# Decoder layer with a selective scan and an int8 feed-forward: gate and up weights measured beside in_proj, rounded inside the scan loop, and turned by transposing transfers

## The chip, the core and the metric

The kernel runs on one core of one Trainium2 chip. A core has TensorE (PE), VectorE (DVE), ScalarE (ACT), GpSimd (POOL), SyncE (SP), which here only issues transfers, and 16 DMA engines. The metric is the device time of one execution in microseconds; lower is better. Each engine runs its own list of instructions in the order in which the program emits them, and waits on semaphores.

## The reference

Two batches of 512 tokens, width 1024, go through three residual parts. Cut to what is computed:

```
# 1: x = x + mixer(layernorm(x))
u, gate = split(h @ W_in.T)                       # 2 x 2048 channels
u = silu(causal_conv4(u) + conv_b)
dt, B, C = split(u @ Wx.T); each rmsnorm'ed
delta = softplus(dt @ Wdt.T + dt_bias)
state = exp(delta * A) * state + (delta * u) * B  # along t, 2048 channels x 16 states
y = (sum_n state * C + u * D_param) * silu(gate)
out = y @ W_out.T
# 2: x = x + fake_quant(layernorm(x)) @ fake_quant(ctx)
# 3: x = x + ffn(layernorm(x)), every operand of a product int8:
s = max(max|t|, rows) / 127;  q = clip(round(t / s)) * s
h = silu(xq @ w_gate_q.T) * (xq @ w_up_q.T)       # 2752 hidden channels
out = h_q @ w_down_q.T
```

The scales of w_gate and w_up (2752 x 1024) are one per hidden channel, those of w_down (1024 x 2752) one per output channel.

## The kernel before

Everything is in channels-by-time tiles of 128 partitions. `mixer` (L42) first normalises the eight token tiles (`ln_stats` L841, `ln_apply` L850 on VectorE), TensorE turns them (L392), and ScalarE and VectorE copy them out (`ln_evac` L598, L855). Then TensorE computes the u half of in_proj of batch 0, 16 chunks of 128 channels of 16 passes each (`u_part` L396); ScalarE applies the first tap of the convolution (L610), VectorE the other three (`conv_rest` L861), ScalarE the silu of a group of four chunks (`u_silu` L618), and TensorE the small product with Wx (`ssm_product` L428), which sits in its list between passes for the gate (`gate_part` L461).

The scan loop has eight groups (two batches of four groups of four chunks) of 16 steps, one per state. In a step ScalarE makes exp(delta*A) (`decay` L652), GpSimd delta*u*B (`times_b` L770), VectorE runs the recurrence along time (`scan` L926), TensorE turns the states (`turn_state` L486), and VectorE (`add_states` L933) or ScalarE and GpSimd (L664, L789) add them up, weighted by C. In between, by step numbers written into the loops, come the rest of in_proj of both batches, the silu of the gate (`silu_gate` L680 to L683, two loads of tables), and the output product. SP loads u back (`load_u` L256, two buffers) and the rows of B (`load_b` L262, a ring of four).

`attend` (L1001) does the second part in staggered stages. In its last two stages it also computes the scales and codes of the first two chunks of w_gate and w_up: loads L1167, maxima `weight_scales` L1440, codes `weight_codes` L1297.

`feed_forward` (L1473) loops over 22 chunks of 128 hidden channels. For a chunk, SP loads both weight tiles (L1606); VectorE takes the row maxima and scales (`scales` L1816), ScalarE the rounded codes (`codes` L1738: the large number ROUND is added, which leaves the integer in the low bits), TensorE turns them in blocks of 128x128 into four PSUM banks (`turn` L1644), and ScalarE and VectorE copy them out to bf16 with ROUND taken off (`copy_out` L1594). The products are 32 passes of 512 columns (`products` L1665), in two banks for the gate and two for up. VectorE scales them (`scale_products` L1836), ScalarE does the silu (L1753), GpSimd the product (L1793), ScalarE the absolute value (`size` L1758), VectorE the running peak (`raise_peak` L1848). The eight row tiles of w_down are taken along in the same way, in three pieces each (`scales_d` L1828, `codes_d` L1745), through one buffer `raw_d`. A short chain behind the loop turns the peaks into the hidden scales; then the hidden values are rounded chunk by chunk, batch 0 on VectorE (L1893, L1897), batch 1 scaled on GpSimd (L1798) and rounded on VectorE, and TensorE runs the down product of batch 0 with all eight banks open (L1712) and that of batch 1 (L1729).

The places of w_down's tiles in the loop are set by a formula, so is the split of the copies:

```
first = t * (OC - 2) // (JT - 1)      # tile t of w_down: piece 0 at chunk first,
wd_at[first] += [(t, 0)]              # pieces 1 and 2 at the next
return u % 3 == 2                     # this copy-out on VectorE, else on ScalarE
```

## Time and profile before

| | us |
|---|---|
| time, median of 3 executions (1770.48 to 1774.33) | 1770.86 |
| the profiled execution's own time | 1774.07 |
| its span | 1772.3 |
| 0 to 186: layer norm, in_proj of batch 0 | 186 |
| 186 to 1171: scan loop | 985 |
| 1171 to 1416: output product, attend | 245 |
| 1416 to 1669: feed-forward loop and the chain behind it | 253 |
| 1669 to 1772: down product | 103 |

Over the span TensorE is busy 1453 us, VectorE 1387, GpSimd 969, ScalarE 848. A stage is bound by the engine that is busy nearly all of it, or by a chain that passes through several; a total says little here, since the stages have different limits. The granted TensorE clock is 0.92 of full on average.

### The profile page before, as it was taken

Reading aid. Unit: us, or ns where it says so; the run is one execution under the profiler, and the core shown is the slowest. Engines: PE = TensorE matmul, PEld = TensorE weight load, DVE = VectorE, ACT = ScalarE, POOL = GpSimd, SP = SyncE. Lnnn points to the kernel's source line nnn. Section 1 sums busy time; section 2 is a strip of 40 time slices with the busy share of each in tenths; the row PEclk is TensorE's granted clock in tenths of the full one; section 3 lists DMA queues with packets and bytes.
Section 4 is the critical chain, followed back from the end, with each engine's and each line's share of the span. In section 5 each row is a group of like instructions: output and inputs, shape, how many; then the busy total and the mean of one; then the engine's idle time right before and its main releaser. Section 6 shows DMA issues by size and latency. Waiting matters only on the chain. (4 is left out here: it accounts for less than half of the span.)

```text
span 1772.3 us, 18711 instructions
## 1 busy us (share of the span) xinstructions
PE 1453.4 (82%) x5879; PEld 774.0 (44%) x5912; DVE 1386.7 (78%) x1748; ACT 847.9 (48%) x1213; POOL 969.1 (55%) x793
## 2 busy tenths in 40 slices
PE   5999578778789877688888887888999379999788
PEld 3444334444444444444444444443444255555333
DVE  4423899989989999999999898953674658888684
ACT  1212556565566446566465565532322467878200
POOL 0000979879779778898988898930000012222530
PEclk8999788989989989679999899998999689999889
DMA  4343221431321321324616516626520234352004
GB/s 152 95 150 128 85 72 54 129 107 36 129 102 58 107 73 41 102 66 160 220 48 213 176 64 212 238 101 231 201 69 27 74 137 178 127 183 92 24 0 166
DMA packets 73676, 205.15 MB, mean 116 GB/s; under 512 B 6800, under 2 KB 24336, under 8 KB 68784
## 3 DMA queue, kind: packets, MB, share of 16 engines
q1 hardware_dynamic: 70416, 188.29, 31.4%
q10 hardware_dynamic: 3168, 15.73, 2.4%
q8 instruction: 46, 0.75, 0.2%
q14 instruction: 46, 0.38, 0.1%
HBM read 176.66 MB, written 27.33 MB: 115 GB/s over the span
## 5 line engine op out<-in xcount | busy, mean ns | idle before, releaser
L931 DVE TENSOR_TENSOR_SCAN hbuf<-decay,hbuf 128x512 f32<-128x512 f32 x512 | 610.7, 1208 | 37.7 <-ACT decay L661 37.7
L661 ACT ACTIVATE decay<-delta,chan_sb 128x512 f32<-128x512 f32 x512 | 350.2, 688 | 414.6 <-DVE hbuf L931 413.7
L499 PE MATMUL turn<-ident,hbuf 128*128 128x128 f32 x2048 | 349.2, 302 | 200.7 <-DVE hbuf L931 164.8
L499 PEld LDWEIGHTS turn<-ident,hbuf 128*128 128x128 f32 x2048 | 262.4, 154 | 478.8 <-DVE hbuf L931 243.0
L945 DVE SCALAR_TENSOR_TENSOR acc<-turn,pn,acc 128x512 f32<-128x512 f32 x360 | 261.9, 728 | 27.5 <-PE turn L499 26.1
L789 POOL TENSOR_TENSOR acc<-acc,part 128x512 f32<-128x512 f32 x120 | 153.1, 1276 | 57.8 <-ACT part L671 57.5
L1793 POOL TENSOR_TENSOR hid<-gs,us 128x512 f32 (+1 forms) x44 | 56.2, 1284 | 194.6 <-ACT gs L1753 181.8
L770 POOL TENSOR_TENSOR hbuf<-wout,sx 128x512 f32<-128x512 f32 x128 | 158.7, 1274 | 0.4 <-POOL wout L778 0.2
L770 POOL TENSOR_TENSOR hbuf<-du,b_more 128x512 f32<-128x512 f32 x128 | 158.9, 1276 | 0.0
L770 POOL TENSOR_TENSOR hbuf<-wout,b_more 128x512 f32<-128x512 f32 x128 | 158.6, 1273 | 0.0
L770 POOL TENSOR_TENSOR hbuf<-du,sx 128x512 f32<-128x512 f32 x128 | 158.5, 1273 | 0.0
L1675 PE MATMUL bank<-codes,wT 128*128 128x512 bf16 (+1 forms) x683 | 153.8, 382 | 1.3 <-ACT wout L1736 0.2
L481 PE MATMUL bank_g<-wout,codes 128*128 128x512 f32 x256 | 136.9, 622 | 0.0
L413 PE MATMUL bank_u<-wout 128*128 128x512 f32 x224 | 118.8, 652 | 0.9 <-DVE wout L858 0.9
L1325 POOL TENSOR_TENSOR rstd<-rstd,mhalf 128x1 f32<-128x1 f32 x16 | 12.9, 807 | 175.4 <-DVE rstd L1364 175.4
L1675 PEld LDWEIGHTS bank<-codes,wT 128*128 128x128 bf16 (+1 forms) x704 | 69.8, 99 | 79.7 <-issue 3.2
L413 PE MATMUL bank_s<-wout 128*128 128x512 f32 x208 | 100.3, 598 | 0.0
L481 PE MATMUL bank_s<-wout,codes 128*128 128x512 f32 x192 | 100.1, 603 | 0.0
L812 POOL TENSOR_TENSOR rs<-rs,mhalf 128x12 f32<-128x12 f32 x2 | 4.5, 2272 | 147.4 <-DVE rs L898 147.4
L671 ACT ACTIVATE part<-turn,pn 128x512 f32<-128x512 f32 x120 | 80.2, 668 | 6.3 <-PE turn L499 6.3
L796 POOL TENSOR_TENSOR y_out<-y_out,gbuf 128x512 f32<-128x512 f32 x32 | 40.6, 1269 | 70.9 <-DVE y_out L923 64.0
L1184 PE MATMUL bank_o<-wout,codes 128*128 128x512 f32 x128 | 58.0, 614 | 3.9 <-PEq L53 3.9
(208 smaller groups left out, 2173.2 us busy)
## 6 DMA issues: line engine op xcount, KB each, us to landing
wout<-in_woutT SPq DMA_DIRECT2D x48, 512.0 KB, 4.2
codes<-in_wg SPq DMA_DIRECT2D x8, 2048.0 KB, 7.7
sx<-bt_scratch SPq DMA_DIRECT2D x64, 256.0 KB, 3.2
b_more<-bt_scratch SPq DMA_DIRECT2D x64, 256.0 KB, 3.4
raw_d<-in_w_down SPq DMA_DIRECT2D x8, 1376.0 KB, 5.7
wout<-in_w_gate SPq DMA_DIRECT2D x21, 512.0 KB, 4.1
wout<-in_w_up SPq DMA_DIRECT2D x21, 512.0 KB, 4.8
wout<-in_wu SPq DMA_DIRECT2D x18, 512.0 KB, 3.5
```

The lines of the kernel that those rows point to most:

```text
L413: last = pe.matmul(u_bank(i)[:, :], w_ring[:, i % 2, k * P:k * P + P], xT[:, k, b * L:b * L + L], start=(k == 0), stop=(k == KC - 1))
L481: mm = pe.matmul(gate_bank(G, j)[:, :], wg_buf[:, k, j * P:j * P + P], xT[:, k, b * L:b * L + L], start=(k == 0), stop=(k == KC - 1))
L499: last = pe.transpose(turn[t % 2][:, j * P:j * P + P], hbuf[:, s % 4, j, t * P:t * P + P], ident[:, :])
L661: act.activation(decay_bank[q % 2][:, :], delta[:, G % 2, j, :], ACT.Exp, scale=a_col(GD * (G % GROUPS) + j, n)).then_inc(dA_done, 1)
L671: act.activation(part[:, k % 2, :], turn[ZT % 2][:, :], ACT.Copy, scale=pn[:, G // GROUPS, ZT, c:c + 1]).then_inc(part_done, 1)
L770: pool.tensor_tensor(hbuf[:, s % 4, j, :], du[G % 2][:, j, :], b_row[s % 4], ALU.mult).then_inc(dbu_done, 1)
L789: pool.tensor_tensor(a, a, part[:, k % 2, :], ALU.add).then_inc(part_added, 1)
L931: dve.tensor_tensor_scan(h, decay_bank[q % 2][:, :], h, 0.0, ALU.mult, ALU.add).then_inc(scan_done, 1)
L945: dve.scalar_tensor_tensor(a, state, pn[:, G // GROUPS, t, c:c + 1], a, ALU.mult, ALU.add)\
L1184: last = pe.matmul(bank_o[w % 2][half][:, :], (keep.yT if w < 2 else yT)[:, w % 2, c, :], wout[:, c, half * 512:half * 512 + 512], start=( ...
L1675: last = pe.matmul(banks[b][0:r, :], wT[:, c % 2, m, k, 0:r], keep.codes[:, k, b * L:b * L + L], start=(k == 0), stop=(k == KC - 1))
L1793: pool.tensor_tensor(hid[0:r, bass.ds(c, 1), b * L:b * L + L], gs[0:r, b:b + 1, :], us[0:r, b:b + 1, :], ALU.mult)\
```

## The change

1. In `mixer`, the first VectorE copies of the turned tiles come before the statistics of tiles 4 to 7.
2. The row maxima of all 44 tiles of w_gate and w_up (22 chunks, two matrices) are taken by VectorE between the convolution taps of batch 0 (`weight_max`), from raw tiles that SP loads through a ring of eight, and all scales are computed there at once.
3. In the scan loop ScalarE rounds these tiles, each in four pieces of 128x512, two that scale and add ROUND and two that take it off into bf16. SP loads each raw tile a second time and stores the bf16 codes to a scratch in memory. To make room, u has one buffer instead of two and is loaded twice a group, and the rows of B have a ring of three.
4. `attend` loses its weight work; at its end SP issues eight transposing transfers, four chunks of two matrices, of 128x1024 bf16 each.
5. The feed-forward loop has no turns on TensorE. Weights arrive turned, four chunks ahead. The product banks alternate between two sets of four. Tiles of w_down are measured at chunk `wd_at`, rounded one iteration of the loop later, made plain bf16 another one later, and turned by one transposing transfer from SBUF to SBUF, behind which the next tile's load stands on SP.
6. The rounding of batch 1 of the hidden values moves from VectorE to ScalarE.

```
+        def units_at(i):
+            at = [2, 0, 2, 2] + [4] * 9 + [2]
+            lo = sum(at[:max(i - 1, 0)])
+            return range(lo, lo + at[i - 1]) if 1 <= i < DC - 1 else range(0)
...
+        QSLOTS = 2 * (STEPS - 8)
+
+        def quant_at(q):
+            return range(4 * UNITS * q // QSLOTS, 4 * UNITS * (q + 1) // QSLOTS) if q < QSLOTS else range(0)
...
+            def load_raw(u):
+                m, c, n = u % 2, u // 2, unit_rows(u)
+                if u >= RAWS:
+                    sp.wait_ge(w_scale, u - RAWS + 3)
+                else:
+                    sp.wait_ge(stat, 4 * (u + 1))
+                sp.dma_start(raw[u % RAWS][0:n, :], (w_gate, w_up)[m][c * P:c * P + n, :]).then_inc(raw_in[u % RAWS], 16)
...
+            def load_quant(u):
+                m, c, n = u % 2, u // 2, unit_rows(u)
+                if u >= 2:
+                    sp.wait_ge(q_step, 4 * (u - 1))
+                else:
+                    sp.wait_ge(w_scale, W_DONE)
+                sp.dma_start(qraw[0:n, u % 2, :], (w_gate, w_up)[m][c * P:c * P + n, :]).then_inc(q_in[u % 2], 16)
...
+            def store_quant(u):
+                m, c, n = u % 2, u // 2, unit_rows(u)
+                sp.wait_ge(q_step, 4 * (u + 1))
+                sp.dma_start(wq_dram[m, c * P:c * P + n, :], qcode[0:n, :]).then_inc(q_stored, 16)
```

In ScalarE's part of the mixer, with the two calls in its loop over steps:

```
+            def quant(q):
+                for o in quant_at(q):
+                    u, half, plain = o // 4, o % 2, o % 4 >= 2
+                    n, c = unit_rows(u), u // 2
+                    v = qraw[0:n, u % 2, half * 512:half * 512 + 512]
+                    if plain:
+                        act.wait_ge(q_step, o - 1)
+                        if u >= 1:
+                            act.wait_ge(q_stored, 16 * u)
+                        act.activation(qcode[0:n, half * 512:half * 512 + 512], v, ACT.Identity, bias=rnd[0:n, 1:2])\
+                            .then_inc(q_step, 1)
+                    else:
+                        act.wait_ge(q_in[u % 2], 16 * (u // 2 + 1))
+                        if u == 0:
+                            act.wait_ge(w_scale, W_DONE)
+                        act.activation(v, v, ACT.Identity, bias=rnd[0:n, 0:1], scale=keep.iw[0:n, u % 2, c:c + 1])\
+                            .then_inc(q_step, 1)
...
+                    quant(2 * s)
...
+                    quant(2 * s + 1)
```

VectorE's part of the mixer:

```
+            def weight_max(u):
+                n = unit_rows(u)
+                dve.wait_ge(raw_in[u % RAWS], 16 * (u // RAWS + 2))
+                dve.tensor_reduce(keep.am[0:n, u % 2, u // 2:u // 2 + 1], raw[u % RAWS][0:n, :], AX_X, ALU.max,
+                                  apply_absolute_value=True).then_inc(w_scale, 1)
+
             for i in range(TT):
                 ln_stats(i)
             for i in range(TT):
                 ln_apply(i)
+            for i in range(TT):
+                ln_evac(2 * i + 1)
             for i in range(TT, TOK // P):
                 ln_stats(i)
-            for i in range(TT):
-                ln_evac(2 * i + 1)
+            dve.memset(rnd[:, 0:1], ROUND)
...
+                        for u in units_at(GD * g + j):
+                            weight_max(u)
                     if g >= 1 and j == 1:
                         add_ssm(g - 1)
+            dve.wait_ge(w_scale, UNITS + 2)
+            dve.tensor_scalar(keep.sw, keep.am, 1.0 / QMAX, SMIN, ALU.mult, ALU.max).then_inc(w_scale, 1)
+            dve.wait_ge(w_scale, UNITS + 3)
+            dve.reciprocal(keep.iw, keep.sw).then_inc(w_scale, 1)
             add_ssm(GROUPS - 1)
```

The feed-forward: the places of w_down, SP, and the order of an iteration on ScalarE and VectorE.

```
+        wd_at = {c: t for t, c in enumerate((0, 3, 6, 9, 11, 14, 17, 20))}
...
+            def load_wT(c):
+                sp.wait_ge(up_mm, 2 * (c - WT) + 2)
+                r = rows(c)
+                for m in range(2):
+                    sp.dma_start(wT[:, c % WT, m, :, 0:r], wq_dram[m, c * P:c * P + r, :], transpose=True)\
+                        .then_inc(wT_load[c % WT], 16)
+
+            def turn_wd(t):
+                sp.wait_ge(wd_plain, NP * (t + 1))
+                if t == 0:
+                    sp.wait_ge(pad_made, 1)
+                sp.dma_start(wdT[:, 0:OC, t * P:t * P + P], code_d[:, :], transpose=True).then_inc(wd_turned, 16)
 
             def load_wd(t):
                 if t >= 1:
-                    sp.wait_ge(block_turned, of["d", t - 1, NP - 1][-1] + 1)
+                    sp.wait_ge(wd_plain, NP * t)
                 sp.dma_start(raw_d[:, :], w_down[t * P:t * P + P, :]).then_inc(wd_load, 16)
...
+                if c + WT < OC:
+                    load_wT(c + WT)
+                if c - 2 in wd_at:
+                    turn_wd(wd_at[c - 2])
+                    if wd_at[c - 2] + 1 < JT:
+                        load_wd(wd_at[c - 2] + 1)
+            turn_wd(JT - 1)
...
+            def plain_d(t, m):
+                act.wait_ge(wd_code, NP * t + m + 1)
+                if m == 0 and t >= 1:
+                    act.wait_ge(wd_turned, 16 * t)
+                act.activation(code_d[:, piece(m)], raw_d[:, piece(m)], ACT.Identity, bias=rnd[:, 1:2]).then_inc(wd_plain, 1)
...
-                if 1 <= c <= OC:
-                    for b in range(BATCH):
+                    if 1 <= c <= OC:
                         silu(c - 1, b)
+                if c - 1 in wd_at:
+                    for m in range(NP):
+                        codes_d(wd_at[c - 1], m)
+                if c - 2 in wd_at:
```

ScalarE's rounding of batch 1 of the hidden values, for each chunk:

```
+                act.wait_ge(q_scaled[1], c + 1)
+                act.activation(v, v, ACT.Identity, bias=rnd[0:r, 0:1]).then_inc(q_rounded, 1)
+                act.wait_ge(q_rounded, c + 1)
+                to = q_space(c - 1, 1)[0:r] if c else q0[0:r, 1:2, :]
+                act.activation(to, v.unsqueeze(1), ACT.Identity, bias=rnd[0:r, 1:2]).then_inc(q_done[1], 1)
```

On VectorE, at the end of in_proj of batch 0: the taps of chunks 13 and 14 (line L868 before, L968 now), with the ssm sum of a group. Before:

```order
L868 SCALAR_TENSOR_TENSOR wout<-bank_s,chan_sb,wout 128x511 [waits conv_start]
L868 SCALAR_TENSOR_TENSOR wout<-bank_s,chan_sb,wout 128x510 [waits conv_tap]
L868 SCALAR_TENSOR_TENSOR wout<-bank_s,chan_sb,wout 128x509 [waits conv_tap]
L878 TENSOR_TENSOR ssm_sum<-bank_m,ssm_sum 96x512 [waits ssm_added,ssm_mm]
L868 SCALAR_TENSOR_TENSOR wout<-bank_g,chan_sb,wout 128x511 [waits conv_start]
L868 SCALAR_TENSOR_TENSOR wout<-bank_g,chan_sb,wout 128x510 [waits conv_tap]
L868 SCALAR_TENSOR_TENSOR wout<-bank_g,chan_sb,wout 128x509 [waits conv_tap]
L868 SCALAR_TENSOR_TENSOR wout<-bank_u,chan_sb,wout 128x511 [waits conv_start]
```

Now, with maxima of weight tiles (L1051), the next rows after chunk 13's taps:

```order
L968 SCALAR_TENSOR_TENSOR wout<-bank_s,chan_sb,wout 128x510 [waits conv_tap]
L968 SCALAR_TENSOR_TENSOR wout<-bank_s,chan_sb,wout 128x509 [waits conv_tap]
L1051 TENSOR_REDUCE row_scales<-du 128x1 [waits x_in6]
L1051 TENSOR_REDUCE row_scales<-du 128x1 [waits x_in7]
L1051 TENSOR_REDUCE row_scales<-acc 128x1 [waits x_in0]
L1051 TENSOR_REDUCE row_scales<-acc 128x1 [waits x_in1]
L978 TENSOR_TENSOR ssm_sum<-bank_m,ssm_sum 96x512 [waits ssm_added,ssm_mm]
L968 SCALAR_TENSOR_TENSOR wout<-bank_g,chan_sb,wout 128x511 [waits conv_start]
L968 SCALAR_TENSOR_TENSOR wout<-bank_g,chan_sb,wout 128x510 [waits conv_tap]
L968 SCALAR_TENSOR_TENSOR wout<-bank_g,chan_sb,wout 128x509 [waits conv_tap]
L1051 TENSOR_REDUCE row_scales<-acc 64x1 [waits x_in2]
L1051 TENSOR_REDUCE row_scales<-acc 64x1 [waits x_in3]
```

The four maxima behind chunk 13's taps stand ahead of the ssm sum and of chunk 14's, and two more behind those.

On ScalarE, steps around the silu of a gate in the scan loop. Before (decay L661, silu L682, scaled state L671):

```order
L661 ACTIVATE decay<-delta,chan_sb 128x512 [waits delta_done,scan_done] x2
L661 ACTIVATE decay<-delta,chan_sb 128x512 [waits scan_done] x2
L671 ACTIVATE part<-turn,pn 128x512 [waits part_added,turned]
L682 ACT_TABLE_LOAD
L682 ACTIVATE gbuf<-gbuf 128x2048 [waits gate_evac]
L683 ACT_TABLE_LOAD
L661 ACTIVATE decay<-delta,chan_sb 128x512 [waits scan_done] x8
L671 ACTIVATE part<-turn,pn 128x512 [waits part_added,turned]
L610 ACTIVATE wout<-bank_u,chan_sb 128x512 [waits ssm_mm,u_stored,w_used]
```

Now (decay L757, silu L778, scaled state L767, the pieces of weight rounding L709 with ROUND added and L703 with it taken off):

```order
L757 ACTIVATE decay<-delta,chan_sb 128x512 [waits delta_done,scan_done] x2
L703 ACTIVATE qcode<-wout,rnd 128x512 [waits q_stored,q_step]
L757 ACTIVATE decay<-delta,chan_sb 128x512 [waits scan_done] x2
L767 ACTIVATE part<-turn,pn 128x512 [waits part_added,turned]
L778 ACT_TABLE_LOAD
L778 ACTIVATE gbuf<-gbuf 128x2048 [waits gate_evac]
L779 ACT_TABLE_LOAD
L757 ACTIVATE decay<-delta,chan_sb 128x512 [waits scan_done] x2
L709 ACTIVATE wout<-wout,rnd,row_scales 128x512 [waits q_in0]
L757 ACTIVATE decay<-delta,chan_sb 128x512 [waits scan_done] x2
L709 ACTIVATE wout<-wout,rnd,row_scales 128x512 [waits q_in0]
L757 ACTIVATE decay<-delta,chan_sb 128x512 [waits scan_done] x2
```

The pieces stand between pairs of decays, one a half step, three times in four.

On SP, the beginning of the feed-forward. Before:

```order
L1614 DMA raw_d<-in_w_down 128x2752
L1609 DMA wout<-in_w_gate 128x1024 [waits block_turned]
L1609 DMA wout<-in_w_up 128x1024 [waits block_turned]
L1614 DMA raw_d<-in_w_down 128x2752 [waits block_turned]
L1609 DMA wout<-in_w_gate 128x1024 [waits block_turned]
L1609 DMA wout<-in_w_up 128x1024 [waits block_turned]
L1609 DMA wout<-in_w_gate 128x1024 [waits block_turned]
L1609 DMA wout<-in_w_up 128x1024 [waits block_turned]
```

Now:

```order
L1683 DMA raw_d<-in_w_down 128x2752
L1671 DMA_TRANSPOSE wout<-wq_scratch 128x8x128 [waits up_mm]
L1671 DMA_TRANSPOSE wout<-wq_scratch 128x8x128
L1671 DMA_TRANSPOSE wout<-wq_scratch 128x8x128 [waits up_mm]
L1671 DMA_TRANSPOSE wout<-wq_scratch 128x8x128
L1671 DMA_TRANSPOSE wout<-wq_scratch 128x8x128 [waits up_mm]
L1671 DMA_TRANSPOSE wout<-wq_scratch 128x8x128
L1678 DMA_TRANSPOSE wout<-code_d 128x22x128 [waits pad_made,wd_plain]
L1683 DMA raw_d<-in_w_down 128x2752 [waits wd_plain]
```

A load of w_down stands behind the turning transfer of the tile before it, and both behind the turned weights of four chunks ahead.

## Rows read from the trace of the kernel before

**Rows 1.** Busy times by stage; share of DMA engines and GB/s last.

```profile
core 0: us, PE busy (x) PEld busy (x) DVE busy (x) ACT busy (x) POOL busy (x), PEclk, DMA share, GB/s
...
186.00:1171.00 985.00, 785.63 (x3160) 432.98 (x3160) 915.25 (x1021) 554.61 (x826) 847.51 (x687) 0.91 0.34 112
...
1416.20:1669.00 252.80, 222.84 (x1251) 136.96 (x1274) 198.94 (x291) 181.00 (x256) 58.55 (x46) 0.95 0.37 131
```

**Rows 2.** Timeline at the start: start, duration, instruction, idle before it and releaser.

```profile
15.78 1.28 DVE L844 BATCH_NORM_STATS2 stats<-hbuf 128x6 f32<-128x512 f32 x2
...
22.28 0.68 DVE L858 COPY wout<-turn 128x512 f32<-128x512 f32 x1
...
23.02 1.11 PE L392 MATMUL turn<-ident,hbuf 128*128 128x128 f32 x4 [4.68 <-DVE wout L858]
...
26.71 2.05 PE L413 MATMUL bank_u<-wout 128*128 128x512 f32 x2 [0.87 <-DVE wout L858]
```

**Rows 3.** Busy times of two stretches, and the timeline at in_proj's end.

```profile
30.00:165.00 135.00, 135.00 (x340) 60.71 (x339) 43.77 (x61) 25.08 (x27) 0.00 (x0) 0.99 0.36 122
...
1176.00:1190.00 14.00, 13.27 (x32) 5.81 (x31) 0.00 (x0) 5.43 (x5) 1.26 (x1) 1.00 0.79 300
...
140.44 2.32 DVE L868 SCALAR_TENSOR_TENSOR wout<-bank_u,chan_sb,wout 128x511 f32<-128x511 f32 x3 [14.93 <-ACT wout L610]
...
156.44 1.91 ACT L618 ACTIVATE wout<-wout 128x2048 f32<-128x2048 f32 x1 [2.38 <-DVE wout L868]
...
159.95 3.60 PE L433 MATMUL bank_m<-wout,wx_buf 128*96 128x512 f32 x8
```

**Rows 4.** VectorE's waits for decay in the scans (total, times, longest), and one.

```profile
DVE hbuf L931 <- ACT decay L661: 37.7, 33, 3.2
...
450.20 1.22 DVE L931 TENSOR_TENSOR_SCAN hbuf<-decay,hbuf 128x512 f32<-128x512 f32 x1 [2.81 <-ACT decay L661]
```

**Rows 5.** Timeline of VectorE at the end of attend.

```profile
1406.56 2.33 DVE L1444 TENSOR_REDUCE row_scales<-wout 128x1 f32<-128x1024 f32 x2
```

**Rows 6.** Groups of the feed-forward loop: busy, mean ns, idle before.

```profile
L1675 PE MATMUL bank<-codes,wT 128*128 128x512 bf16 x651 | 146.8, 382 | 1.3 <-ACT wout L1736 0.2
...
L1657 PE MATMUL bank<-ident,wout 128*128 128x128 f32 x336 | 43.4, 286 | 2.3 <-DVE wout L1859 2.3
...
L1820 DVE TENSOR_REDUCE row_scales<-wout 128x1 f32<-128x1024 f32 x38 | 44.3, 1208 | 0.0
...
L1846 DVE SCALAR_TENSOR_TENSOR us<-bank,row_scales,sx 128x512 f32<-128x512 f32 x42 | 31.3, 744 | 13.0 <-PE bank L1675 13.0
...
L1855 DVE TENSOR_TENSOR wout<-wout,us 128x512 f32<-128x512 f32 x42 | 27.2, 687 | 2.9 <-ACT us L1758 2.9
...
L1830 DVE TENSOR_REDUCE amd<-raw_d 128x1 f32<-128x2752 f32 x8 | 24.0, 3004 | 3.8 <-DMA raw_d<-in_w_down 3.8
...
L1748 ACT ACTIVATE raw_d<-raw_d,rnd,isd 128x1024 f32<-128x1024 f32 x16 | 19.7, 1234 | 13.0 <-DVE isd L1834 13.0
```

**Rows 7.** DMA: issues, KB, landing time; then the queue from 1194 to 1202.

```profile
raw_d<-in_w_down SPq DMA_DIRECT2D x8, 1376.0 KB, 5.7
...
yT_scratch<-y_out SPq DMA_DIRECT2D x4, 256.0 KB, 2.3
...
q1 hardware_dynamic: 2036, 1.02, 43.5%
```

**Rows 8.** The last peak, and the first down product after it.

```profile
1658.82 0.69 DVE wout L1855
...
1669.04 3.19 PE L1712 MATMUL bank<-wout,q 128*128 128x512 bf16 x7 [3.77 <-DVE q L1897]
```

**Rows 9.** The chain and the timeline while hidden values are rounded.

```profile
1666.66 32.90 POOL L1798 TENSOR_TENSOR hid<-hid,wout 128x512 f32 x22 [8.54 <-ACT wout L1786]
...
1674.32 1.76 DVE hid L1893
...
1700.13 27.86 PE L1712 MATMUL bank<-wout,hid 128*128 x120 [2.58 <-DVE hid L1897]
```

374 lines of the change are left out of this document (147 added, 227 removed).

## The prediction, made before the changed kernel ran

> **What bounds the kernel now.** I read the busy times by stage first. From 186 to 1171 us the scans on VectorE set the time: 915 of 985 us busy, ScalarE 555, GpSimd 848. In the feed-forward loop, 1416 to 1669, TensorE is busy 223 of 253 us, with VectorE (199) and ScalarE (181) close behind [rows 1]. In in_proj, ahead of the scans, TensorE alone is full, and VectorE has 44 us of work in 135 [rows 3]. So work leaves the stage where three engines are full, and lands in one full on TensorE alone and in one full on VectorE. Next I read the timelines of the places where the edits sit, then the waits within the scans, then the groups of the loop.
>
> **Start.** TensorE is idle for 4.68 us before its turning at 23.02, released by VectorE's copy at 22.28; that copy stands behind sixteen statistics instructions of tiles 4 to 7, which begin at 15.78 [rows 2]. The new order puts the four copies first, at 15.9 instead of 22.3, and the statistics beside the products. The first product (26.71) comes about 6 us earlier; behind it the next thing late would be its weights, whose loads are issued with the inputs. **-6** (0 to -6.5).
>
> **In_proj.** VectorE gets 44 row maxima. One of 1024 columns takes 1.21 us [rows 6], so 53 us, and the stretch has 91 us free on VectorE, while TensorE has no gap [rows 3]. On average it fits. At the end it doesn't: conv_rest of chunks 12 and 13 begins at 140.44 (2.32 a chunk), u_silu starts at 156.44 as chunk 15's taps end and takes 1.91, and ssm_product stands at 159.95 behind gate passes [rows 3]. In the new order VectorE still has, from 140.44, four chunks' taps, ten maxima and the addition of one ssm sum (0.7): 140.44 + 4 x 2.32 + 10 x 1.17 (their pace back to back) + 0.7 = 162.1, silu to 164.0, ssm_product at 164.1, 4.1 us late. Three of gate_part's steps instead of one follow it, two more of 0.86, +1.7. So +6. A lag of VectorE carried from earlier groups and transfers come on top. Four raw tiles and one of in_proj's, 0.524 MB each, in a chunk's 6.86 us are 382 GB/s; the busiest stretch that I found moved 300 GB/s at a DMA share of 0.79, that is 380 at a full one [rows 3]. The weights of in_proj queue behind the raw tiles on one queue. I take +3 for this (0, as VectorE paces the raw loads, to 20, if nine chunks run at two thirds of their speed). **+9** (6 to 27).
>
> **Scan loop.** ScalarE gets 176 pieces of 128x512. ScalarE's codes_d takes 1.23 us for 1024 columns [rows 6], so 0.62 a piece and 109 us, and ScalarE has 430 us free there [rows 1]. The pieces lie between decays. VectorE waits 33 times for a decay, 37.7 us in all; the worst are at silu_gate, 2.81 us at 450.20 [rows 4]. A piece ahead of the awaited decay lengthens such a wait by at most 0.62. Three quarters of the half steps have a piece, so 33 x 0.62 x 0.73 = 15 if none is absorbed, and new short waits beside. **+10** (3 to 20). What hides the rest is ScalarE's idle time, and its pieces are issued behind decays of the same step, which are ready first. The loads and stores (22 + 11 MB over 900 us) are nothing for the queues; with a three-deep b_row ring a transfer still has two steps, of 985/128 = 7.7 us, ahead of its use.
>
> **Attend.** VectorE's maxima of the last stage, 2.33 us at 1406.56, stand between the last statistics and the last normalising [rows 5]; GpSimd's rstd covers 0.8 of it. **-2** (-1 to -3). The eight transposing transfers (0.26 MB each) stand on SP ahead of store_x2(7), where four raw loads of 0.52 MB stood. At 2.3 us, as y_out's stores of 0.26 MB [rows 7], eight cost what the four did, so nothing; if each were 2 us longer the last store and the stage's end would wait.
>
> **Feed-forward loop.** TensorE loses its turns of the gate and up weights (43.4 us) and of w_down, and keeps the products: 146.8 us in 651 of 704 passes, 7.0 or less a chunk, 154 in all [rows 6]. If the rest kept up, the loop would go down to that. It doesn't, because w_down goes round in a ring of one buffer: load, maximum, codes one iteration later, plain codes another iteration later, turning transfer, and the next load is issued behind that transfer on the same queue. VectorE stands in the next maximum until the load lands, and all iterations stand with it. One round:
> load 5.7 [rows 7]; maximum 3.0 and two small ones 0.4; the next chunk's two peaks and four scalings (2 x 0.69 + 4 x 0.74), 4.4, of which 3.3 are ahead of ScalarE's last silu of 0.6, so 3.9; codes_d 3.3 (2752 columns at 1.23 per 1024); the chunk after 4.5 (4.4 and a lag); plain_d 3.4, priced like it; issue 0.4; turning transfer T; semaphores' lags 0.8, an estimate [rows 6, 7]. That is 25.4 + T.
> T is the cost no row shows. It moves 0.72 MB. As a plain transfer by bytes it is 5.7 x 0.72/1.41 = 2.9. By packets: 256-byte pieces are 2816, 176 for each of 16 engines; the stores of y_out in 512-byte packets cost 0.435 x 16 x 8 us / 2036 = 27.4 ns each [rows 7], which gives 4.8. Below, 0 if it hides under the load. I take 3.0, the nearer row in size of transfer, and keep 0 and 4.8, and ten or more for smaller pieces.
> The Trainium skill (Advanced Engine Details and Errata, X-Bar Transpose) says that on trn2 transposing DMAs are as fast as plain ones; with the row of 5.7 us that is the 2.9 above. No run here shows it yet.
> Seven rounds of 28.4 are 199, 3 ahead of the first, and 24 from the last load's issue to the last peak (5.7 + 3.4, two chunks of 7.0 and their silu): 226. The chain behind the last peak (turning peaks, inverse, spreading, first codes) stays 9.5, from 1659.51 to 1669.04 [rows 8]. 236 against 252.8 [rows 1]: **-17**. It moves with T by 8 us a microsecond (eight transfers): -41 at 0, -3 at 4.8.
> Without the PE's pauses GpSimd's multiply and VectorE's peak stand closer in time and share their lock: I add **+3** (0 to 6).
>
> **Down.** GpSimd's 22 scalings of batch 1 take 32.90 us, 1.50 each, and meanwhile VectorE's multiply of 128x512 lasts 1.76 us where its maximum of two such tiles takes 0.69 [rows 6, 9]: each of VectorE's three instructions a chunk waits out one of GpSimd's, 4.5 us a chunk. With batch 1's rounding on ScalarE there are two, 3.0 a chunk: by GpSimd's end 11 chunks are done instead of 7, and the PE's 120 remaining passes at 232 ns [rows 9] are fewer by 3.7 x 8 = 29, 6.9 us; a bit more at the start. **-8** (-3 to -12). ScalarE's pieces for batch 1 (1.2 a chunk) keep pace with GpSimd and are done long before 1728.
>
> **Sum.** -6 + 9 + 10 - 2 - 17 + 3 - 8 = -11. The profiled execution took 1774.07 (span 1772.3), 3.2 above the median of 1770.86. 1774.07 - 11 = 1763 on its own scale, 1760 on the median's. I say 1761.
>
> **Rivals.**
> 1. Turning transfers are dear (ends slower). Loop and total move by 8 x (T - 3.0), so the whole gain is gone at T = 4.4. At 4.8 (27.4 ns for 256 bytes) the total is +3; at pieces of 128 bytes for the same 27.4 ns T is 9.6 and the total +42, 1813. For it: the packet price hardly falls with size in the rows. Against: nothing in the rows shows this kind of transfer. 0.22, around 1790.
> The Trainium skill's page VectorE: DVE Perf Modes (The three transpose paths) gives 1309 ns for one 128x128 block by DMA and advises TensorE where the result may go to PSUM. By it, if blocks did not overlap, T would be an estimated 29 us; no run here shows it, and it is the case of rival 2.
> 2. The 128x128 blocks run one after the other, each near what a small transfer takes here (2.3 us for 256 KB [rows 7], about 1 for 32 KB). 16 a chunk and 22 a piece of w_down on one queue are 22 x 16 + 8 x 22 = 528 us, the total +280, 2040. 0.03.
> 3. The mixer gives it back: the transfers of in_proj bind (27 instead of 9) and the pieces go fully onto VectorE's waits (20 instead of 10). -11 + 28 = +17, 1788. For it: 382 GB/s wanted of 380. Against: VectorE's own pace throttles the raw loads. 0.16.
> 4. The round is shorter, the transfer running beside the next load and the iterations overlapping: 25 us a round, another -24, 1737 to 1740. For it: the queue serves 16 engines and 5.7 us include a fixed part. 0.12.
> 5. The terms cancel, T near 4: 1767 to 1774. 0.07.
>
> **Numbers.** My forecast, 1752 to 1768, has 0.40. What a measurement can tell from no change is 0.2%, 3.5 us. Faster: 0.36 of the forecast, 0.12 of 4, 0.02 of 5: 0.50. Same: 0.04 + 0.05 of 5 + 0.01 of 3: 0.10. Slower: 0.22 + 0.03 + 0.15: 0.40. The range leaves out 1813 and the upper part of rival 1, rival 2, and little below: 1738 to 1803.
>
> **What would show it.** First product at about 20.5 instead of 26.7. ssm_product of the last group within 5 to 8 us of 160 + 4 - 6. Stage of the scans 988 to 1005 us, VectorE's wait for decay 41 to 58. Each w_down round 27 to 30, VectorE's idle ahead of the w_down maximum named DMA, one turning transfer about 3 us from issue to landing. Loop 236, TensorE idle a third of it. Batch 0's codes at 3.0 us a chunk. I am wrong if a turning transfer takes over 4.4 us, if SP is busy long with issuing one, or if TensorE waits for wT instead of VectorE for w_down.

## The result: 0.9% slower, and where the 12.3 us of the span went

The changed kernel takes 1787.94 us (median of 4, 1786.22 to 1794.10), the kernel before takes 1772.59 (median of 4). The ratio is 1.0092, 95% interval 1.0061 to 1.0123. I had forecast 1761, 11 us faster than before; faster had a chance of 0.50, slower 0.40. The time lies inside my range, but on the slower side.

The profiled execution of the changed kernel spans 1784.6 us (1786.35 its own time), 12.3 more than before's. Busy times by stage, as in [rows 1], cut at the same events (first scan, end of the scans, issue of the first load of w_down, first down product):

```profile
core 0: us, PE busy (x) PEld busy (x) DVE busy (x) ACT busy (x) POOL busy (x), PEclk, DMA share, GB/s
0.00:188.20 188.20, 154.47 (x400) 71.47 (x400) 117.97 (x164) 40.88 (x52) 12.29 (x16) 0.98 0.69 251
188.20:1188.80 1000.60, 791.14 (x3160) 434.57 (x3160) 915.96 (x1021) 670.44 (x1002) 848.28 (x687) 0.90 0.45 151
1431.30:1687.80 256.50, 179.66 (x744) 79.39 (x744) 138.00 (x166) 102.09 (x142) 57.90 (x47) 0.86 0.45 107
1687.80:1784.60 96.80, 81.24 (x352) 33.78 (x352) 64.81 (x74) 30.68 (x44) 31.83 (x21) 0.98 0.22 76
```

Against [rows 1]: in the scans VectorE's work is the same (916 against 915) in 16 us more; in the feed-forward all three engines have less to do, TensorE 180 instead of 223, and the stage is nevertheless 3.7 us longer. A stage in which every engine is idle for a good part is set by a chain of waits. By events, the span's difference is this sum:

| stage | forecast | measured |
|---|---|---|
| start (its effect on the first scan, from the run with this part alone, below) | -6 | -8.4 |
| in_proj, to the first scan | +9 | +10.6 |
| scans, first to last | +10 | +15.6 |
| attend | -2 | -2.7 |
| feed-forward loop and its chain | -14 | +3.7 |
| down | -8 | -6.5 |
| sum | -11 | +12.3 |

Two terms are off by much: the scans by 5.6 us and the feed-forward by 17.7, of 23.3 in all. The chain of waits there, one round of a w_down tile (start, us, what):

```profile
1489.39 3.31 SPq L1678
1492.69 0.04 issue
1492.74 6.35 DMA raw_d<-in_w_down
1499.08 0.02 issue
1499.11 3.03 DVE amd L1855
...
1502.43 0.70 DVE wout L1880
...
1503.26 0.76 DVE gs L1868
...
1504.05 0.63 ACT gs L1792
1504.67 0.53 ACT us L1797
...
1505.23 1.41 DVE wout L1880
...
1507.55 0.63 ACT gs L1792
1508.18 3.13 ACT raw_d L1781 x3
1511.30 0.53 ACT us L1797
1511.83 0.02 issue
1511.86 0.70 DVE wout L1880
...
1517.50 2.95 ACT code_d L1787 x3
1520.45 0.02 issue
1520.47 3.31 SPq L1678
```

The round is the predicted one in kind: load, maximum, codes, plain codes, turning transfer, load. The eight maxima start at 1437.6 to 1654.6, so seven rounds take 217.0 us, 31.0 each, not 28.4. By parts:

| part of a round | forecast | measured |
|---|---|---|
| load | 5.7 | 6.35 |
| maximum with its small ones | 3.4 | 3.25 |
| from there to the codes | 3.9 | 5.7 |
| codes | 3.3 | 3.1 |
| from there to the plain codes | 4.5 | 6.2 |
| plain codes | 3.4 | 2.95 |
| issue and turning transfer | 3.4 | 3.35 |
| lags | 0.8 | 0.1 |

The two iterations in between are what I mis-sized, by 3.5 us a round; the rows show why. Peak (L1880), scaling (L1868), silu (L1792) and absolute value (L1797) follow each other to and fro between VectorE and ScalarE, since the absolute value lies in the buffer that the next scaling overwrites; I had added VectorE's instructions as if they ran back to back. I call this to and fro the handshake. And each second peak takes 1.41 us, twice the 0.69 of [rows 6]. GpSimd's multiply runs beside just that one: a round earlier, the peak of the same place starts at 1483.56 and takes 1.42 us, and GpSimd's multiplies are these:

```profile
1483.15 1.27 POOL L1833 TENSOR_TENSOR hid<-gs,us 128x512 f32<-128x512 f32 x1 [4.64 <-ACT gs L1792]
1486.65 1.27 POOL L1833 TENSOR_TENSOR hid<-gs,us 128x512 f32<-128x512 f32 x1 [2.23 <-ACT gs L1792]
```

### The profile page after: what moved, and what is told of

It reads as the page before. It is cut to its first block and busy times, and to the rows that moved or that the text cites. A ratio compares the mean times of both kernels' runs of the same rounds, so it can differ in the third digit from the quotient of the medians.

```text
span 1784.6 us, 17613 instructions
## 1 busy us (share of the span) xinstructions
PE 1407.0 (79%) x5384; PEld 714.3 (40%) x5384; DVE 1363.5 (76%) x1642; ACT 911.0 (51%) x1314; POOL 970.5 (54%) x794
## 3 DMA queue, kind: packets, MB, share of 16 engines
q1 hardware_dynamic: 152208, 247.54, 42.8%
## 5 line engine op out<-in xcount | busy, mean ns | idle before, releaser
L757 ACT ACTIVATE decay<-delta,chan_sb 128x512 f32<-128x512 f32 x512 | 348.6, 687 | 318.8 <-DVE hbuf L1031 317.3
L1045 DVE SCALAR_TENSOR_TENSOR acc<-turn,pn,acc 128x512 f32<-128x512 f32 x360 | 263.0, 731 | 29.2 <-PE turn L577 27.8
L868 POOL TENSOR_TENSOR hbuf<-du,sx 128x512 f32<-128x512 f32 x172 | 213.1, 1275 | 2.0 <-DMA sx<-bt_scratch 2.0
L868 POOL TENSOR_TENSOR hbuf<-wout,sx 128x512 f32<-128x512 f32 x172 | 213.4, 1277 | 0.4 <-POOL wout L878 0.2
L1724 PE MATMUL bank<-codes,wout 128*128 128x512 bf16 (+1 forms) x704 | 171.1, 407 | 52.6 <-DVE gs L1868 51.6
L1833 POOL TENSOR_TENSOR hid<-gs,us 128x512 f32<-128x512 f32 (+1 forms) x44 | 55.8, 1269 | 187.2 <-ACT gs L1792 187.2
L1724 PEld LDWEIGHTS bank<-codes,wout 128*128 128x128 bf16 (+1 forms) x704 | 71.7, 104 | 151.9 <-issue 82.1
L491 PE MATMUL bank_u<-wout 128*128 128x512 f32 x224 | 111.8, 618 | 3.3 <-DMA wout<-in_wu 2.4
L1434 POOL TENSOR_TENSOR rstd<-rstd,mhalf 128x1 f32<-128x1 f32 x16 | 12.9, 807 | 174.8 <-DVE rstd L1473 174.8
L868 POOL TENSOR_TENSOR hbuf<-du,b_more 128x512 f32<-128x512 f32 x84 | 104.4, 1278 | 0.0
L868 POOL TENSOR_TENSOR hbuf<-wout,b_more 128x512 f32<-128x512 f32 x84 | 104.3, 1279 | 0.0
L1792 ACT ACTIVATE gs<-gs 128x512 f32<-128x512 f32 (+1 forms) x44 | 27.6, 630 | 135.6 <-DVE gs L1868 135.6
L1880 DVE TENSOR_TENSOR wout<-wout,us 128x512 f32<-128x512 f32 (+1 forms) x44 | 45.3, 1030 | 65.6 <-ACT us L1797 65.6
L767 ACT ACTIVATE part<-turn,pn 128x512 f32<-128x512 f32 x120 | 80.3, 669 | 6.3 <-PE turn L577 6.3
```

Source lines behind the costliest of these rows:

```text
L491: last = pe.matmul(u_bank(i)[:, :], w_ring[:, i % 2, k * P:k * P + P], xT[:, k, b * L:b * L + L], start=(k == 0), stop=(k == KC - 1))
L757: act.activation(decay_bank[q % 2][:, :], delta[:, G % 2, j, :], ACT.Exp, scale=a_col(GD * (G % GROUPS) + j, n)).then_inc(dA_done, 1)
L767: act.activation(part[:, k % 2, :], turn[ZT % 2][:, :], ACT.Copy, scale=pn[:, G // GROUPS, ZT, c:c + 1]).then_inc(part_done, 1)
L868: pool.tensor_tensor(hbuf[:, s % 4, j, :], du[G % 2][:, j, :], b_row[s % 3], ALU.mult).then_inc(dbu_done, 1)
L1045: dve.scalar_tensor_tensor(a, state, pn[:, G // GROUPS, t, c:c + 1], a, ALU.mult, ALU.add)\
L1724: last = pe.matmul(banks(c, b)[0:r, :], wT[:, c % WT, m, k, 0:r], keep.codes[:, k, b * L:b * L + L], start=(k == 0), stop=(k == KC - 1))
```

## The experiments

The ratio is always to the runs of the kernel before on the same chip, with its 95% interval; a kernel that ran only once has no ratio. Gains in microseconds are against the changed kernel unless the text says otherwise. Rounds are counted from maximum to maximum of w_down's tiles.

**The next load ahead of the turning transfer**

```
-                    turn_wd(wd_at[c - 2])
                     if wd_at[c - 2] + 1 < JT:
                         load_wd(wd_at[c - 2] + 1)
+                    turn_wd(wd_at[c - 2])
```

> The changed kernel, with the next load of w_down issued ahead of the turning transfer of the tile before it instead of behind it. Theory A (the w_down round sets the loop, and the 3.3 us for which SP is held while it issues the turning transfer are part of it, since the next load stands behind): the round goes from 31.1 to 27.8 us, seven rounds give -23, time about 1765. Theory B (the transfers themselves share the queues: whichever is first, load and turning transfer together take the 9.7 us that they take now): the load lands as late as now, no change, 1788. Theory C (the iterations' own handshakes set the pace and the load's wait is only what is left over): at most -5, 1783.

1765.14 us, ratio 0.9959 (0.9941 to 0.9976). In its chain the load follows ScalarE's plain codes at once. The round shown takes 27.8 us (1467.57 to 1495.39), the seven average 27.5:

```profile
1467.57 3.03 DVE amd L1855
...
1485.95 2.95 ACT code_d L1787 x3
1488.92 6.45 DMA raw_d<-in_w_down
1495.39 3.03 DVE amd L1855
```

Theory A, to the microsecond. SP now needs 6.61 us to issue the turning transfer behind the load, and nobody waits for it.

**The pieces in ScalarE's gaps**

```
                     if c >= 2:
                         size(c - 2, b)
+                    for m in ((0,), (1, 2))[b]:
+                        if c - 1 in wd_at:
+                            codes_d(wd_at[c - 1], m)
+                        if c - 2 in wd_at:
+                            plain_d(wd_at[c - 2], m)
                     if 1 <= c <= OC:
                         silu(c - 1, b)
-                if c - 1 in wd_at:
-                    for m in range(NP):
-                        codes_d(wd_at[c - 1], m)
...
```

> The changed kernel, with ScalarE's rounding pieces of w_down (three that add ROUND, three that take it off, a round) no longer behind the second silu of an iteration and ahead of the next absolute value, but between absolute value and silu, where ScalarE is idle for 1.6 us (first half) and 2.4 us (second half) in every iteration: one piece in the first half, two in the second. Theory A (the pieces stand in the chain of the round, 3.1 + 2.95 us of it): the round goes from 31.1 to 25 to 26 us, -36 to -43, time about 1750. Theory B (the load and the SP queue set the round, ScalarE's pieces are beside it): within 5 us of 1788. Theory C (TensorE or the iterations at 7 us each become the bound at once): -20.

1749.52 us, ratio 0.9879 (0.9855 to 0.9903): the time of theory A, 38 us less. The seven rounds average 27.1 us, against 31.0 and the 25 to 26 of the theory. The stage from the first load of w_down to the first down product is some 31 us shorter; the other 7 us of the profile lie in its scan loop, which the edit doesn't touch (992.6 against 999.4 us from first to last scan; this loop varies from profile to profile). ScalarE's timeline shows what the gap takes in; its idle ahead of the two silus is 0.25 and 0.35 us behind pieces that add ROUND, where the changed kernel has 1.64 and 2.35:

```profile
1519.74 0.63 ACT L1792 ACTIVATE gs<-gs 128x512 f32<-128x512 f32 x1 [0.25 <-DVE gs L1867]
1520.28 0.61 ACT L1797 ACTIVATE us<-hid 128x512 f32<-128x512 f32 x1
1520.80 2.10 ACT L1781 ACTIVATE raw_d<-raw_d,rnd,isd 128x1024 f32<-128x1024 f32 x2
1523.25 0.63 ACT L1792 ACTIVATE gs<-gs 128x512 f32<-128x512 f32 x1 [0.35 <-DVE gs L1867]
```

**Both**

> Both edits: the load ahead of the turning transfer, and the pieces in ScalarE's gaps. Theory A: the gains add until TensorE's 7 us a chunk bind (2.75 chunks a round, 19.3): round 21.8, -60, time 1725 to 1735, TensorE busy in over 80% of the loop. Theory B (something else, such as the handshake of VectorE and ScalarE at 6 us or more an iteration plus 3.2 for the maximum, takes over): round 24 to 25, time about 1745.

1730.49 us, ratio 0.9773 (0.9750 to 0.9796). The rounds average 24.2 us (first maximum 1433.7, last 1603.0): the time of theory A, the round of theory B. The gains add nearly in full: the same stage is some 23, 31 and 52 us shorter in the three kernels. TensorE still waits 18.5 us for scalings; the next edit takes up the handshake.

**The peak apart**

```
-                act.activation(us[0:r, b, :], hid[0:r, c, b * L:b * L + L], ACT.Abs).then_inc(size_done, 1)
+                if c >= 1:
+                    act.wait_ge(peak_done, 2 * (c - 1) + b + 1)
+                act.activation(mag[0:r, b, :], hid[0:r, c, b * L:b * L + L], ACT.Abs).then_inc(size_done, 1)
...
-                    dve.wait_ge(peak_done, 2 * (c - 1) + b + 1)
                 dve.scalar_tensor_tensor(gs[0:r, b, :], bank_gate(c, b)[0:r, :], sw[0:r, 0, c:c + 1], sx, ALU.mult, ALU.mult)\
...
-                dve.tensor_tensor(v, v, us[0:r, b, :], ALU.max).then_inc(peak_done, 1)
+                dve.tensor_tensor(v, v, mag[0:r, b, :], ALU.max).then_inc(peak_done, 1)
...
                 for b in range(BATCH):
-                    if c >= 2:
-                        raise_peak(c - 2, b)
                     if 1 <= c <= OC:
                         scale_products(c - 1, b)
+                for b in range(BATCH):
+                    if c >= 2:
+                        raise_peak(c - 2, b)
```

> The changed kernel, with the absolute value of a hidden tile written to a buffer of its own instead of over the up product, so that VectorE's scalings of the next chunk no longer stand behind the peak (which waits for ScalarE's absolute value); in an iteration VectorE now does the four scalings first and the two peaks after them. Nothing else is changed. Theory A (the prediction failed in the two iterations of a w_down round, 5.8 and 6.2 us by the handshake of VectorE and ScalarE against the 3.9 and 4.5 summed from busy times): codes start 3.6 us after the maximum, plain codes 2.3 us after the codes, the round goes from 31.1 to about 25, time about 1745. Theory B (the handshake is only what fills the time until the next load, and the load and SP set the round): round above 30, time 1780 or more.

1747.31 us (1741.46 to 1753.68), ratio 0.9830 (0.9793 to 0.9867): theory A. The rounds average 25.9 us, and the stage is 42.8 us shorter. The edit separates the buffers and, on VectorE, also puts the peaks behind the scalings; the two can't be told apart here. GpSimd's collisions stay (the peaks' mean is 1284 ns), so it is not those that the gain comes from. The shortest round, 23.7 us, here VectorE's part, with scalings back to back and the peaks behind them:

```profile
1503.72 3.02 DVE L1858 TENSOR_REDUCE amd<-raw_d 128x1 f32<-128x2752 f32 x1 [7.12 <-DMA raw_d<-in_w_down]
...
1507.04 0.75 DVE L1870 SCALAR_TENSOR_TENSOR gs<-bank,row_scales,sx 128x512 f32<-128x512 f32 x1
...
1509.02 0.74 DVE L1873 SCALAR_TENSOR_TENSOR us<-bank,row_scales,sx 128x512 f32<-128x512 f32 x1
1509.68 2.42 DVE L1882 TENSOR_TENSOR wout<-wout,mag 128x512 f32<-128x512 f32 x2
...
1527.44 3.02 DVE L1858 TENSOR_REDUCE amd<-raw_d 128x1 f32<-128x2752 f32 x1 [4.94 <-DMA raw_d<-in_w_down]
```

ScalarE starts the codes 2.9 us after this maximum and the plain codes 2.0 us after the codes (3.6 and 2.3 had been expected, 5.7 and 6.2 were the changed kernel's).

**All three**

> All three edits of the feed-forward together: next load ahead of the turning transfer, rounding pieces in ScalarE's gaps, peak apart. With the first two the loop takes 23 to 25.5 us a round at 2.75 chunks, TensorE waits 18.5 us for scalings. Theory A (the handshake is still part of it): the rounds fall to 20 to 22, -10, 1720, TensorE's waits for scalings under 10 us. Theory B (already bound by TensorE and VectorE's own work): within 3 us of 1730.

1719.63 us (5 runs), ratio 0.9672 (0.9653 to 0.9690): 3.3% faster than before and the best kernel of this study. The time is theory A's; the rounds average 22.7 us and TensorE still waits 12.9 us for scalings, both a little more than it said (20 to 22, under 10). VectorE waits 39.5 us for the load of w_down. The loop isn't bound by TensorE even here.

**One block in place of 22**

```
-                sp.dma_start(wdT[:, 0:OC, t * P:t * P + P], code_d[:, :], transpose=True).then_inc(wd_turned, 16)
+                sp.dma_start(wdT[:, 0:1, t * P:t * P + P], code_d[:, 0:P], transpose=True).then_inc(wd_turned, 16)
```

> The changed kernel, with the turning transfer of each w_down tile cut from 22 blocks of 128x128 to one (the down product's values are then wrong; its buffer is set to zero once by GpSimd at the loop's start). SP is held for 3.31 us by 22 blocks and for 1.25 by 8, about 0.15 a block. Theory A (issue time in proportion to blocks, and the next load waits for that): SP's issue falls to 0.2 to 0.4 us, the round from 31.1 to 27.5 to 28, total -20. Theory B (the load behind it also lands sooner because the turning transfer's pieces no longer share the queue, 6.35 to 5.7): a further 0.6 a round, total -25.

1771.97 us in one run, 16 us less. The rounds average 29.2 us and the stage is 12 us shorter, less than either theory, since SP is still held for 1.12 us by a single block:

```profile
1488.17 1.12 SPq L1678 DMA_TRANSPOSE wout<-code_d  x1
1489.33 0.58 SPq L1683 DMA_DIRECT2D raw_d<-in_w_down  x1
```

Between one block and 22, a block costs SP 0.10 us on average, (3.31 - 1.12)/21. That is no rule for other transfers: the eight-block ones from memory hold SP for a median of 1.31 us, where it would give 1.8, and with the load ahead the same 22 blocks hold it for 6.6. SP's time thus depends on what the queue is doing, and how is open. The load lands in 6.3 us (median) as before: no theory B.

**Parts 1 and 6 undone in the changed kernel**

```
-            for i in range(TT):
-                ln_evac(2 * i + 1)
             for i in range(TT, TOK // P):
                 ln_stats(i)
+            for i in range(TT):
+                ln_evac(2 * i + 1)
...
-            hid_codes(0, 0, q0[:, 0:1, :])
+            for b in range(BATCH):
+                hid_codes(0, b, q0[:, b:b + 1, :])
...
```

> The changed kernel, with two parts undone: the first copies of the turned tiles stand again behind the statistics of tiles 4 to 7, and the rounding of batch 1 of the hidden values is again on VectorE. Theory A (each part gives what the prediction says, alone): first product back from 20.68 to 26.7, the down stage back from 96.8 to 103.3 us, 4.5 us a chunk, total +12. Theory B (in_proj waits for its weights and maxima in any case, so that a later start is absorbed): the first product is later but ssm_product of the last group stays at 160 to 163, and the total is +7.

1801.91 us in one run, span 1800.1, 15.5 longer than the changed kernel's. The first product is at 26.93, the first scan 8.3 us later (196.56), VectorE again takes 4.48 us a chunk (1699.41 to 1703.89), and the down stage is some 5 us longer; the scan loop, not touched, has the other 2. Theory A, with a start that is worth more than I gave it.

**Part 1 alone, in the kernel before**

> The kernel before, with only the first part of the change: the first copies of the turned tiles ahead of the statistics of tiles 4 to 7. Theory A (TensorE's list simply starts 6 us earlier and nothing else is late): first product at 20.6 instead of 26.7, first scan at 180, time -6, ratio 0.9966. Theory B (the second batch of statistics and the tiles 4 to 7 behind them come too late, or weights do): first scan at 183 or later, ratio 0.998 to 1.

1764.93 us, ratio 0.9957 (0.9940 to 0.9974), -7.6 us; first scan 8.4 us earlier. 5.8 of it is the earlier first product (20.95 against 26.71), the rest is TensorE's clock. The stretch of the first 17 passes, of before and of this kernel, in that order (columns as in the result's first rows):

```profile
26.70:36.40 9.70, 9.69 (x17) 4.21 (x18) 0.00 (x0) 0.00 (x0) 0.00 (x0) 0.73 0.00 0
```

```profile
20.90:28.10 7.20, 7.15 (x17) 3.34 (x18) 6.13 (x16) 0.01 (x1) 0.72 (x1) 1.00 0.00 0
```

Before, TensorE had idled for 4.68 us just ahead of its second turnings [rows 2]. It was granted 0.50 of 2.4 GHz, which is 1.2 GHz, from 23.0 to 26.7 us, and 0.73 on average over these passes, so part of them ran at 1.2 GHz too; without the gap it is 1.00.

**One-column pieces in the scan loop**, in the changed kernel and in the one of 1730.49 us:

```
-                    v = qraw[0:n, u % 2, half * 512:half * 512 + 512]
+                    v = qraw[0:n, u % 2, half * 512:half * 512 + 1]
...
```

> The changed kernel, with the 176 rounding pieces in the scan loop cut to one column each (the loads, stores and waits stay; the weights of gate and up are then not the right codes, and the feed-forward's values are left out of consideration). The stretch from the first to the last scan grew from 983.8 to 999.4 us, 15.6. Theory A (the pieces delay decays that VectorE waits for): 11 to 13 of the 15.6 go, VectorE's wait for decay falls from 50 to about 38 us. Theory B (the extra transfers, the single buffer of u and the shorter ring of B rows do it): the stretch stays at 997 or more.

> The kernel of 1730.5 us (load first, pieces in the gaps) with the 176 rounding pieces of the scan loop cut to one column (gate and up codes are then wrong). Seven profiles of the same scan loop vary between 992.6 and 1002.5 us from first to last scan, and one profile with tiny pieces had 992.8, so the price of the pieces' length has to come from whole times. Theory A (their length costs 5 to 8 us, by VectorE's waits for decay, 50 against 43 us): 1723 to 1725. Theory B (the difference of the profiles was chance): 1729 to 1732.

First: 1777.97 us in one run, first to last scan 992.8, 6.6 less than the changed kernel's 999.4: neither theory's. Second: 1726.54 us, ratio 0.9722 (0.9704 to 0.9740), against 1730.49 and 0.9773 (0.9750 to 0.9796) with full pieces. The intervals are just apart; the pieces' length costs 4 us by the two times and 9 by the two ratios, which are of different chips, so about what theory A says. First to last scan is 992.7. Only 7 us of the wait for decays follow the pieces' length; with full and with tiny pieces:

```profile
DVE hbuf L1031 <- ACT decay L757: 50.3, 33, 3.8
```

```profile
DVE hbuf L1031 <- ACT decay L757: 43.2, 32, 3.4
```

[rows 4] had 37.7, in 33 waits, and a second profile of the kernel before 38.9 in 31. So a wait is some 0.15 us longer with pieces of any length, and another 0.2 by the pieces' length.

**Small transfers, alone and with one-column pieces**

```
-                sp.dma_start(qraw[0:n, u % 2, :], (w_gate, w_up)[m][c * P:c * P + n, :]).then_inc(q_in[u % 2], 16)
+                sp.dma_start(qraw[0:2, u % 2, :], (w_gate, w_up)[m][c * P:c * P + 2, :]).then_inc(q_in[u % 2], 16)
...
-                sp.dma_start(ubuf[:, :, :].rearrange("p j t -> p (j t)"), u_dram[G]).then_inc(u_in, 16)
+                n = 2 if again else P
+                sp.dma_start(ubuf[0:n, :, :].rearrange("p j t -> p (j t)"), u_dram[G][0:n]).then_inc(u_in, 16)
```

> The changed kernel, with the transfers that the change adds to the scan loop made small: the second loads of the raw gate and up tiles bring 2 rows instead of 128, the second loads of u 2 rows of 128 (codes and y are then wrong); ScalarE's pieces keep their full size, with a small scale in place of the right one. With one-column pieces the first-to-last-scan stretch was 992.8 us, against 999.4 of the changed kernel and 983.8 of before, so 6.6 us hang on the pieces' length and 9.0 on something else. Theory A (half of the 9.0 is the transfers: in the last group TensorE waits for output weights that queue behind them, and VectorE for TensorE): the stretch is 993 to 996, the 4 us lost between scans 480 and 496 are gone. Theory B (the rest is ScalarE's fixed cost of a piece and its waits, transfers are nothing): the stretch stays at 999.

> The changed kernel with one-column pieces and small added transfers at once (2 rows of 128 of each raw tile and of each second load of u; codes and y are then wrong). First to last scan: 983.8 before, 992.8 with one-column pieces alone. Theory A (transfers: output weights late in the last group and B rows late behind them): 985 to 988. Theory B (fixed costs of 176 pieces and their waits on ScalarE): 990 to 993.

Alone: 1783.36 us in one run, first to last scan 997.8, between the two theories and within the spread of this loop's profiles (below). Together: 1771.61 us in one run, first to last scan 986.1, 6.7 less than with tiny pieces alone: theory A. What holds in every profile is the end of the loop: its last 32 scans take 50.2 to 50.4 us in the kernel before and wherever these transfers are small, and 52.2 to 54.7 in all others, so the transfers cost 2 to 4 us there. Part of it is TensorE's wait for output weights, in the changed kernel

```profile
PE bank_u L602 <- DMA wout<-in_woutT: 10.0, 6, 3.6
```

against 4.1 us in 3 waits before, 5.5 in 6 with the transfers small and 4.2 in 4 with pieces and transfers small.

**The kernel before again, and with a ring of three**

```
-                    if s + 4 < STEPS:
-                        load_b(s + 4)
+                    if s + 3 < STEPS:
+                        load_b(s + 3)
...
```

> The kernel before, unchanged, for a second profile of its scan loop: the first gave 983.8 us from first to last scan, and the seven profiles of the changed loop vary by 10 us. If before varies likewise (983 to 993) the scan loop's price of 15.6 us was partly chance and is nearer 10; if it is 982 to 986 the price is 9 to 19, mean 14.5.

> The kernel before, with a ring of three rows of B in place of four, nothing else. Theory A (a ring of three is enough, as the prediction took it: two steps of 7.7 us for a landing of 3.2 to 3.8): first to last scan 983.5 to 985, GpSimd never waits for a B row. Theory B (it is part of the open 9 us): 986 or more, with GpSimd waits named DMA.

One run each. Before again: 1776.35 us, first to last scan 983.9, so the kernel before doesn't vary as the changed one does. Ring of three: 1775.08 us, first to last scan 987.5, with a first scan 2.7 us earlier; GpSimd waits once for a row of B, 2.1 us. These are theory B's signs, but the last scan ends only 1.1 us later than before's, and one profile doesn't settle it. With pieces and transfers small, 2.3 us of the 16 are left (986.1 against 983.8); they may be the ring's.

**Pieces moved away from the silu of the gate**

```
+            if q >= QSLOTS or (q // 2) % N < 2:
+                return range(0)
...
-            at = [2, 0, 2, 2] + [4] * 9 + [2]
+            at = [2, 0, 3, 3] + [4] * 8 + [3, 1]
```

> The kernel with both edits of the feed-forward (load first, pieces in ScalarE's gaps), and two more: ScalarE's rounding pieces of gate and up leave out the first two steps of each group, where VectorE waits for decays behind the silu of the gate, and end with the seventh group, ahead of the last one, where output weights were late; and two of the row maxima move away from the last two chunks of in_proj. Theory A (pieces next to the table loads and transfers next to the output weights cost 8 of the 15.6 us): 1720 to 1725. Theory B (a denser row of pieces in the other steps costs as much as it saves): 1730.

1732.41 us, ratio 0.9772 (0.9756 to 0.9789), as without: theory B. VectorE's wait for decays is 50.6 us, no less. The three moves were made at once, so the run shows that together they give nothing, not that each gives nothing.

## Why the prediction was wrong, step by step

- *Start, -6.* Right in its mechanism, too small: -8.4, because the gap had also cost TensorE clock.
- *In_proj, +9.* +10.6. ssm_product of the last group came at 160.5, near the 158 and a lag of 3 that the terms give. I gave VectorE's late end with the gate steps 6 and the transfers 3; it is the other way round, and that the sum came out near is luck: TensorE waited 2.4 and 3.9 us for in_proj's own weights, behind raw tiles in the queue,

```profile
137.40 8.83 PE L491 MATMUL bank_g<-wout 128*128 128x512 f32 x16 [3.86 <-DMA wout<-in_wu]
```

  and 2.0 us for VectorE, half of it by way of ScalarE's silu. The two more gate steps cost 1.7 as priced. The 380 GB/s that I took for a full queue is not its limit: from 20 to 26.7 us the changed kernel moves 404.
- *Scan loop, +10 (3 to 20).* +15.6 in this profile. Eight profiles of this same loop range from 992.6 to 1008.3 us, mean 1000.5, against 983.8 and 983.9 of before: +17 on average. By the profiles with tiny pieces and small transfers, some 8 of it are the pieces' length and some 7 the added transfers; each share rests on one or two profiles of a loop that varies by as much, and only the 2 to 4 us at its end stand in all of them. "The loads and stores (22 + 11 MB over 900 us) are nothing for the queues" was the part that failed: I compared bytes with time, and not which transfer stands behind which, where TensorE waits for output weights in the last group. What spreads the changed loop over 16 us, and not the loop before, stays open.
- *Attend, -2.* -2.7.
- *Feed-forward loop, -17.* This is the step that failed: the round of w_down, in "the next chunk's two peaks and four scalings ... so 3.9" and "the chunk after 4.5". That is 8.4 us where 11.9 were measured, since I summed busy times and left out the waits of the handshake. Of the 3.5 us, 1.4 are two slow peaks (below), the other 2.1 are waits. Seven rounds of 3.5 are 24 us, against which the round's other parts came out 6 smaller. The last two chunks add to it in the same way: from the last load's issue to the last peak's end it is 29.7 us (1648.1 to 1677.8), where I had 24. Against that, the 3 us that I put ahead of the first load are not there.
- *The turning transfer T.* In the chain its cost came out as forecast, 3.31 us against 0.4 and 3.0, but not for the reason that I gave, and so by luck. I took T for the time of the transfer on the queue. By my own signs I was wrong: a turning transfer takes 5.2 us from issue to landing, over the 4.4 that I had named, and SP is busy long with issuing one. The next load doesn't wait for the landing but for SP, and SP is held for 3.3 us. Rivals 1 and 2 had the place, not the cost. The queue is idle for the first 1.1 us of the issue, and then moves the transfer in 3.3 us, until 1.2 us behind the issue's end; from 1489 to 1494 us, in 40 slices:

```profile
GB/s 0 0 0 0 0 0 0 0 0 0 0 0 43 199 227 215 217 221 211 197 211 221 221 217 217 215 217 217 229 205 225 213 221 217 215 213 227 193 197 574
```

  The Trainium skill (Advanced Engine Details and Errata, X-Bar Transpose) has it that such transfers are as fast as plain ones. This trace doesn't agree: from 1490.7 to 1493.8 us the turning transfer moves 215 GB/s, and the first load of w_down, with the queue to itself, 309 from 1432.3 to 1436.7. It is nearer in the kernel that issues the load first, where 290 are moved behind the load, from 1495.4 to 1497.2. The 1309 ns for a block that the Trainium skill's page VectorE: DVE Perf Modes (The three transpose paths) gives does not add up over the blocks of one transfer: 22 landed 5.2 us after issue, one alone 2.3.
- *GpSimd's lock, +3.* Right in kind, too small. Its size is in the rounds: the peaks' mean is 1030 ns instead of 687, 15 us in all; two slow peaks a round stand in the chain, 1.4 us, so 10 of the 24 us in seven rounds. I had 3.
- *Down, -8.* -6.5; batch 0's codes took 3.08 us a chunk, 3.0 had been said.
- *Rival 3* (the mixer gives it back, +17 by 47 us in in_proj and scans): 26.2 were measured, 19 forecast. Not the cause: with start and attend the mixer's side is +15.1, and with -17 from the loop and -6.5 from down the change would still have been 8 us faster. With the loop repaired it is 56 (1775.37 to 1719.63).

## What to carry to other kernels

When engines hand a buffer to and fro, price the path through the hand-overs, one instruction after another in the order of the waits, and not the busiest engine's sum; and look for what stands in an engine's list between two instructions of that path, since moving it into a gap a few microseconds away was worth some 31 us here. A transfer's bytes against a queue's free time say nothing on the transfers behind it: ask which one is needed next. In a ring of one buffer, issue the next load first, and everything that only uses what was read out of it afterwards.

## What the runs showed that I had not expected

- Issuing a turning transfer holds SP: 3.31 us for 22 blocks from SBUF, 1.12 for one, a median of 1.31 for eight from memory, against 0.34 for a plain transfer (0.58 right behind a turning one). With a load just ahead, the 22 blocks hold it for up to 6.99.
- A gap of 4.68 us ahead of TensorE's turnings cost 2.6 us of clock in the 16 passes after them, 9.7 instead of 7.1 us.
- VectorE's maximum of two tiles takes 0.69 us alone and 1.41 with GpSimd's multiply of the same size beside it.
- The same scan loop, with transfers and pieces added, varies by 16 us from profile to profile; without them three profiles (of the kernel before, twice, and with part 1 alone) lie between 983.6 and 983.9.
